# Message layer of a graph network: edge tiles gathered once into a ring of 64 places, and read slot by slot

## What is computed

```
m_in = concat([h[src], h[dst], edge_attr])          # 64 + 64 + 32
m    = silu(m_in @ w1 + b1) @ w2 + b2
agg  = segment_sum(m, dst)
upd  = silu(concat([h, agg]) @ w3 + b3) @ w4 + b4
x    = x + layernorm(h + upd) * gamma + beta
```

## Time and profile before

| | us |
|---|---|
| time of the runs | 2219.85 median of 3 (2215.54 to 2220.22) |
| span of the profiled execution | 2219.0 |
| its GpSimd busy | 1464.2 (66%) |
| its TensorE busy (matmul) | 1463.9 (66%) |
| its VectorE busy | 986.6 (44%) |
| its ScalarE busy | 478.2 (22%) |
| mean granted TensorE clock | 0.629 of full speed |

### The profile page before, as it was taken

How to read it: one execution, slowest core, us unless ns; L and a number is a source line. 1 busy time by engine, 2 the same in 40 slices (tenths; PEclk the granted TensorE clock), 3 DMA queues, 4 the chain that set the end, 5 groups by cost and what they waited for, 6 DMA issues and landing times.

```text
span 2219.0 us, 27516 instructions
## 1 busy us (share of the span) xinstructions
PE 1463.9 (66%) x8192; PEld 1339.9 (60%) x8192; DVE 986.6 (44%) x3043; ACT 478.2 (22%) x1108; POOL 1464.2 (66%) x1534
## 2 busy tenths in 40 slices
PE   6343333333569999986888898989483337657783
PEld 3243333333569899985778887888453327656673
DVE  6321111111488988846323333333432235455687
ACT  4100000000068887802010101010221111111120
POOL 2577777777377777752777777777127777777750
PEclk9655555555578988857555555555666557656687
DMA  7623131313112222212333333332073323323220
GB/s 252 208 54 102 27 101 26 83 27 73 27 34 46 47 42 46 42 20 59 62 69 62 69 63 69 62 69 48 5 279 80 76 75 81 81 72 85 67 65 15
DMA packets 153942, 159.41 MB, mean 72 GB/s; under 512 B 102042, under 2 KB 105674, under 8 KB 152829
## 3 DMA queue, kind: packets, MB, share of 16 engines
q0 software_dynamic: 49152, 70.29, 15.0%
q1 hardware_dynamic: 104652, 87.36, 14.0%
HBM read 120.58 MB, written 44.36 MB: 74 GB/s over the span
## 4 chain that ended last, share of the span: by engine, by line
POOL 64%; issue 21%; PE 5%; DVE 5%; DMA 4%; SPq 1%; ACT 0%; POOLq 0%; DVEq 0%; ACTq 0%
POOL flat L555 45%; POOL flat L547 18%; DMA table<-flat 2%; PE ps L1265 1%; PE ps L1460 1%; DMA flat<-table,flat 1%; PE ps L1206 1%; PE ps L1197 1%; PE ps L1222 1%; DVE var L635 0%; PE ps L1408 0%; DMA flat<-table,tile_idx 0%; DVE uvT L628 0%; DVE mean L626 0%; PE ps L1417 0%
## 5 line engine op out<-in xcount | busy, mean ns | idle before, releaser
L555 POOL DMA_INDIRECT flat<-table,flat x694 | 665.7, 959 | 271.8 <-issue 210.6
L1265 PE MATMUL ps<-flat,oh 128*128 x1664 | 320.7, 373 | 340.6 <-DMA flat<-table,flat 315.9
L749 DVE TENSOR_SCALAR oh<-iota_n,drel 128x128 f32<-128x128 f32 x1248 | 265.8, 302 | 618.0 <-PE ps L1265 426.6
L1265 PEld LDWEIGHTS ps<-flat,oh 128*128 128x128 f32 x1664 | 305.0, 284 | 355.7 <-issue 353.8
L547 POOL DMA_INDIRECT flat<-table,flat x416 | 400.8, 964 | 178.6 <-issue 126.5
L555 POOL DMA_INDIRECT flat<-table,tile_idx x391 | 378.0, 967 | 205.8 <-issue 118.6
L1408 PE MATMUL ps<-qn,ohT 128*128 x832 | 169.2, 387 | 104.8 <-DVE ohT L755 100.9
L1234 PE MATMUL ps<-msg,oh 128*128 128x64 f32 x832 | 187.1, 418 | 69.6 <-ACT msg L1119 69.6
L1247 PE MATMUL ps<-uvT,flat 128*128 128x192 bf16 x2200 | 217.0, 267 | 16.3 <-ACT flat L1100 15.3
L1408 PEld LDWEIGHTS ps<-qn,ohT 128*128 128x128 f32 x832 | 159.0, 294 | 111.1 <-issue 110.8
L1234 PEld LDWEIGHTS ps<-msg,oh 128*128 128x128 f32 x832 | 177.5, 324 | 78.6 <-issue 78.6
(11 more groups left out here) (285 smaller groups left out, 1251.9 us busy)
## 6 DMA issues: line engine op xcount, KB each, us to landing
table<-flat SPq DMA_DIRECT2D x52, 512.0 KB, 4.4
drow<-slot_node SPq DMA_DIRECT2D x104, 256.0 KB, 3.5
flat<-table,flat POOLq DMA_INDIRECT x1110, 2.5
flat<-edge_attr_by_slot SPq DMA_DIRECT2D x52, 128.0 KB, 3.9
flat<-table,tile_idx POOLq DMA_INDIRECT x391, 2.6
edge_attr_padded<-edge_attr SPq DMA_DIRECT2D x1, 6250.0 KB
flat<-tile_source SPq DMA_DIRECT2D x22, 256.0 KB, 3.3
edge_attr_by_slot<-flat SPq DMA_DIRECT2D x2, 2048.0 KB, 6.9
```

Source lines behind the costliest of these rows:

```text
L555: nc.gpsimd.indirect_dma_start(dest(t % PLACES), None, table, at_).then_inc(tile_gat[k % TRING], 16)
L749: last = V.tensor_scalar(oh[:, b, j, :], iota_n[:], drel[:, bass.ds(g * SG + j, 1)], None, ALU.is_equal)
L1265: last = T.matmul(acc[:, bass.ds(n[j] * pitch + shift, width)], oh[:, b % 2, j, :], got[:, bass.ds(place[j], width)], start=False, stop=Tr ...
```

## The change

The message layer gathers the 391 edge tiles once each, as the other layers do, into `got0` (64 places at a pitch of 65 values). GpSimd waits, from group 8 on, for VectorE's add of slot group g-5. VectorE waits for tile group g while g < 49, loads eight places, and adds slot by slot, from `eb` and the ring into `msg`; ScalarE's Silu works in place in `msg` and no longer waits for `used` itself. `idx1` per slot, its transposes and its copy, and the copy of the sources into work[0] go. `tile_idx1` gets a room of its own in place of `idx1`, 25 values shorter, so that what is allocated behind it moves by 100 bytes.

```diff
-        idx1 = early(P, [SLOTS], i32)
+        tile_idx1 = early(P, [TE], i32)
...
-        tile_idx1 = ea_room[:, 0:TE].bitcast(i32)
...
             pool.wait_ge(s("plain_table_out"), 64)
-            for g in range(G):
-                if g >= RING:
-                    pool.wait_ge(s("used"), 2 * G + g - RING + 3)
-                gather(2, g, table2_d[:, :], got1, idx1)
+            for g in range(TG):
+                if g >= TRING:
+                    pool.wait_ge(s("edge_sum"), g - TRING + 3 + 2)
+                gather_tiles(2, g, table2_d[:, :], lambda p: got0[:, p, 0:D], tile_idx1)
...
-            src_, dst_ = (pack[:, :, j, :] for j in range(2))
-            link(V.tensor_copy(work[0], src_))
+            dst_ = pack[:, :, 1, :]
...
-            dve.wait_ge(s("work_T"), 5)
-            link(V.tensor_copy(idx1, aux[:, 0:SLOTS]))
             segment_bounds()
...
                 dve.wait_ge(s("eb_ps"), g + 3)
-                landed(dve, 2, g, b)
-                V.tensor_tensor(got1[:, b], eb[b % 2].rearrange("p (s d) -> p s d", s=SG), got1[:, b], ALU.add).then_inc(s("edge_sum"), 1)
+                if g < TG:
+                    tiles_landed(dve, 2, g)
+                place = slot_places(DVE_, g)
+                for j in range(SG):
+                    last = V.tensor_tensor(msg[:, b % 2, j, :], eb[b % 2][:, j * D:(j + 1) * D], got[:, bass.ds(place[j], D)], ALU.add)
+                last.then_inc(s("edge_sum"), 1)
...
                 act.wait_ge(s("edge_sum"), g + 2)
-                act.wait_ge(s("used"), 2 * G + g + 1)
-                A.activation(msg[:, b % 2], got1[:, b], ACT.Silu).then_inc(s("silu"), 1)
+                A.activation(msg[:, b % 2], msg[:, b % 2], ACT.Silu).then_inc(s("silu"), 1)
...
-            rows_to_columns(0, work[0], START)
             clear_sums()
```

More of the change, by code:

```diff
@@ L182, in network @@
         got0 = got.rearrange("p (t d) -> p t d", d=W)
-        got1 = got[:, 0:RING * SG * D].rearrange("p (b s d) -> p b s d", b=RING, s=SG)
         assert TRING * SG >= TN + 4 * SG and PLACES * W >= 6 * SC * P and TE <= SC * P
@@ L295, in network @@
             s(name)
-        gat = [s(f"gathered{b}") for b in range(RING)]
         tile_gat = [s(f"tiles_gathered{b}") for b in range(TRING)]
@@ L303, in network @@
         INIT, INIT_W = 6, 4
-        NB = G // RING
         assert G % RING == 0
@@ L352, in groups @@
                 step(g, g % RING, G - g)
-        def landed(eng, l, g, b):
-            eng.wait_ge(gat[b], ((l - 2) * NB + 1) * PER + (g - b) * (PER // RING))
         BIG, FAR = 1e38, 2.0 ** 20
@@ L383, in network @@
         block = ctx.enter_context(nc.Block())
-        PER = SG * 16
         WEIGHTS = []
@@ L541, in _ @@
                 nc.gpsimd.indirect_dma_start(dnext[0:n, c, :], None, dst_d[:, :], at_, element_offset=2).then_inc(s("packed"), 16)
[L543 to L547, removed]
             pool.wait_ge(s("tables_made"), 1)
@@ L590, in _ @@
                     pool.wait_ge(s("values"), k - TRING + 3 + 1)
-                gather_tiles(2, k, table3_d.rearrange("n (r d) -> (n r) d", d=2 * D), lambda p: got3[:, p, :], tile_idx3)
+                gather_tiles(3, k, table3_d.rearrange("n (r d) -> (n r) d", d=2 * D), lambda p: got3[:, p, :], tile_idx3)
         @block.vector
@@ L945, in score @@
                 if g < TG:
-                    tiles_landed(dve, 2, g)
+                    tiles_landed(dve, 3, g)
                 dve.wait_ge(s("scored"), g + 2)
@@ L1144, in step @@
                     if g < TG:
-                        tiles_landed(act, 2, g)
+                        tiles_landed(act, 3, g)
                     if c == 2:
```

## The result

The kernel after took 2208.68 us, the median of five runs (2206.75 to 2210.85), beside 2219.85 of the kernel before on the same chip (five runs, 2214.45 to 2223.89). The ratio is 0.9956, with an interval of 0.9941 to 0.9971: faster by 0.3 to 0.6%. Forecast were 2211.8, in a range of 2204 to 2217. The profiled execution took 2206.75 us, of which 2204.9 are the span, at a mean granted clock of 0.622.

The account below looks back on a forecast made before the run. GpSimd's gathers were taken to pace the message layer, TensorE right behind. A gain of 8.7 us less 0.6 for slower gathers gave 8.1: 2219.0 to 2210.9, plus 0.85 for the median, 2211.8 us; range 2204 to 2217.

Parts of the forecast that it names:

- The pace: Message layer up to slot group 48: VectorE waits by tile group, so groups stay 10.07 us apart.
- 25 gathers at 1.26 us: Message layer: 416 gathers become 391, saving 31.5 us of GpSimd, so the last gather starts at 1529.2.
- less 0.6: Message layer gathers: VectorE's extra busy time slows each by 0.0015 us, 0.6 us over 391.
- The tail: Message layer behind the last gather: sums of slot groups 48 to 51 at TensorE's pace, ending 1559.9 instead of 1568.6.
- loads: VectorE, message layer: eight registers loaded behind the gather wait cost 0.8 us, paid once at slot group 48.
- adds: VectorE, message layer: eight 128x64 adds in a row take 1.14 us, replacing one 128x512 add of 0.69.
- Rival B: Message layer's tail: TensorE's clock rises, the layer ends 9.6 us earlier still, 2202.2 us; chance 0.09.
- Rival A: Message layer's tail: its three groups still take 10.07 us each, gain 0.05, 2219.8 us; chance 0.17.
- D: Message layer: it ends the full 31.5 us earlier, 2188.4 us; chance 0.02.
- Rival C: Message layer: VectorE's small instructions slow each gather by 0.066 us, 26 us in all, 2237 us; chance 0.06.

Follow-up runs that it names:

- chip 13: The unedited kernel after run again on the chip also used for the one-add, edge-matmul and looser-wait kernels: 2207.8 us, ratio 0.9950.
- first trace: Profiled execution of the kernel after from its first measurement, no further edit: 2206.75 us, where the median of five runs was 2208.68.
- the waits of `needed` and early loads: Kernel after, all four gather layers waiting only for tile groups each slot group needs, message-layer registers loaded before the waits: 2171.36 us, ratio 0.9795.

## Why the prediction was right

Its mechanism is shown, not only its number. The kernel after gained 11.2, 11.6 and 8.3 us in the three comparisons (forecast 8.1), of which the layer's traces have 10.9, 9.0 and 10.0. Its steps one by one:

- The pace. "Up to slot group 48 the pace is still 10.07 us per group": adds 10.12 us apart, and the pace doesn't move when TensorE has 1.5 us less per group. Shown.
- 25 gathers at 1.26 us: forecast 31.5 less 0.6, measured 526.38 - 495.95 = 30.4 (mean of three). Against 25 x 1.268, the kernel before's own mean, the gathers are 0.6 to 2.0 us slower in sum. I put that on the small adds; the kernel with one add has it too (496.00), so the term was of the right size for a wrong reason, which was luck. What sets it I can't say beyond that the phase of VectorE's large instructions moves it.
- The tail. At the lower clock (chip 13) against the forecast, from the last gather's start: first sum at 5.58 (5.5), second at 14.48 (14.6), third at 23.01 (23.4), end at 30.09 (30.7). Every step is within 0.6 us. The small terms: loads 0.60 in the chain and 0.71 to 0.77 between the kernels with and without them, for 0.8; adds 1.14 for 1.14. The prediction calls 217 ns the time of one small add alone; it is the mean of adds in a row, whose times overlap, and the sum doesn't use it. The estimate of 1.79 us for the adds, worked out from the Trainium skill's "VectorE: DVE Perf Modes" (section "The TRN2 errata — SBUF-src ops pay a fixed extra latency per instruction"), doesn't hold for eight in a row.
- Rival B came in part, in two of three tails. In the first trace the clock was 1.00 from 1544.10 to 1549.76 and 0.53 in the mean of the stretch behind it; its tail is 3.3 us shorter than that of chip 13, though its last landing was 0.9 us later. On chip 13 TensorE worked without a pause from 1532 to 1557 at 0.50 throughout. The Trainium skill's rule that sustained activity releases the clock ("TensorE: Matmul & The Clock Gate", section "Part 1: The HAM clock gate (the "warmup" mystery)") therefore doesn't say which tail gets it. In that first trace the clock is most of the 3.9 us by which the tail is shorter than forecast.
- Rival A is out: in the tail at the lower clock the sums start 8.9 and 8.5 us apart, not 10. D is out, and the kernel with fewer gathers spread over the layer shows what it would have given, 2185.
- Rival C is the one I sized by the wrong thing. I weighed how busy VectorE is and how short its instructions are. The kernel with small adds alone, with 21 us of extra work on VectorE (forecast 23) and no fewer gathers, loses 16 us in the gathers by phase: its one-hots fall just ahead of a gather. The kernel after, with the same adds, has them just behind one. My chance of 0.06 for C rested on a trend over four windows that couldn't show this. I had the direction right partly by luck, because the phase fell well: the 0.7 us of loads, counted as a cost, are what moved the one-hots past the gather's start. Sixteen us would have eaten the gain of ten.

## What to carry to other kernels

Where a consumer waits for groups in order and its producer is made to do less, the saving shows only at the end unless the waits follow what each group reads; count the groups that stay behind the last landing, and loosen the wait before the work. Load what a group needs to know ahead of its wait, where it costs nothing. And when a change moves an instruction by half a microsecond on VectorE, look in the trace where its large instructions now fall beside GpSimd's DMA writes: here the phase cost more (16 us) than the instructions that were added (0.4 us in the tail).

## What the runs showed of the hardware

- A gather of 0.94 us takes 1.30 to 1.46 when a 0.74 us VectorE instruction (128x1024 from bf16) has started 0.10 to 0.26 us earlier. When VectorE's has started 0.09 us earlier or less, the gather keeps its 0.94. When the gather starts 0.53 us ahead it keeps its 0.94 too and VectorE's takes 0.93; when it starts 0.20 to 0.44 us ahead it takes 1.06 to 1.30.
- Eight adds of 128x64 in a row took 1.14 us, one of 128x512 took 0.69; eight registers loaded behind a wait added 0.6 to 0.8 us to the way from landing to add, and none when they were loaded ahead of it.
- One chip ran the kernel before in 2739 us instead of 2220, with TensorE idle between single matmuls. The kernel after with the waits of `needed` and early loads, 2% under the kernel before on another chip, was 1.5% above it there, while fewer gathers gained alike on both (0.9860 and 0.9851). Whether the change itself gains on that chip wasn't run.
